# Two causal attentions on one core: GPSIMD masks the diagonal of the first and sums one tile in four of a head of the second

## The reference

```python
xn = layernorm(x)
x = x + attention(xn, wq, wk, wv, wo) + ternary_mlp(xn, W_up, W_gate, W_down)
xn = layernorm(x)
x = x + gated_cumsum(xn, Wq, bq, ...) + attention_two(xn, Wa, Wp, w_std, w_rec)
```

```python
scores = einsum('bhqd,bhkd->bhqk', q, k) * scale
scores = where(causal, scores, -inf)
out    = einsum('bhqk,bhkd->bhqd', softmax(scores), v)
```

## Time and profile before

| what | us |
|---|---|
| median of 3 runs | 2696.15 |
| lowest and highest of them | 2688.54, 2734.21 |
| the profiled execution, its own time | 2693.72 |
| its span, from first to last instruction | 2692.0 |

### The profile page before, as it was taken

The page is one execution under the profiler, slowest core; times in us unless marked ns, Lnnn a source line. Parts: engine busy times, 40 slices in busy tenths (PEclk is TensorE's granted clock), DMA queues, the critical chain, the costliest instruction groups (busy, mean ns, idle before and its releaser), DMA issues. The chain is left out here.

```text
span 2692.0 us, 42224 instructions
## 1 busy us (share of the span) xinstructions
PE 2394.0 (89%) x16394; PEld 1498.7 (56%) x16394; DVE 1749.8 (65%) x2066; ACT 1249.9 (46%) x2372; POOL 566.8 (21%) x480
## 2 busy tenths in 40 slices
PE   4959999969999999999999869979969999999947
PEld 2748888846555444444444347758745555555515
DVE  3745444555767878888886043422259999999954
ACT  2422222204555767777788522212215655656531
POOL 1110000030000000000000002220036766666650
PEclk8979999977999999999999889989989999999978
DMA  3771000034321211000000020015562222220024
GB/s 123 238 231 48 32 32 31 0 62 85 82 61 38 58 45 30 30 30 21 29 18 15 13 67 1 0 48 116 192 145 47 51 65 65 65 63 10 8 67 144
DMA packets 133182, 168.60 MB, mean 63 GB/s; under 512 B 60736, under 2 KB 70592, under 8 KB 129920
## 3 DMA queue, kind: packets, MB, share of 16 engines
q1 hardware_dynamic: 129536, 153.45, 21.5%
q10 hardware_dynamic: 3456, 12.58, 1.5%
HBM read 114.19 MB, written 51.64 MB: 62 GB/s over the span
## 5 line engine op out<-in xcount | busy, mean ns | idle before, releaser
L710 ACT ACTIVATE a_ex<-a_ps_s 128x512 f32<-128x512 f32 (+3 forms) x1280 | 620.0, 532 | 331.3 <-PE a_ps_s L793 249.3
L913 DVE TENSOR_REDUCE a_mx_part<-a_ps 128x2 f32<-128x1024 f32 (+3 forms) x576 | 584.0, 1043 | 132.2 <-PE a_ps L739 129.7
L1206 ACT ACTIVATE a_ex<-a_ps_s 128x512 f32<-128x512 f32 (+3 forms) x640 | 318.3, 532 | 285.9 <-PE a_ps_s L1267 160.3
L793 PE MATMUL a_ps_s<-a_q,a_k 50*128 50x512 f32 (+3 forms) x1152 | 395.9, 419 | 2.8 <-ACT a_ex L710 2.8
L1181 POOL TENSOR_TENSOR a_acc<-a_acc,a_ex 128x512 f32<-128x512 f32 (+3 forms) x288 | 352.0, 1222 | 95.8 <-ACT a_ex L1206 75.0
L739 PE MATMUL a_ps<-a_k,a_q 48*128 48x512 f32 (+3 forms) x1152 | 346.0, 418 | 27.4 <-DVE a_low_q L898 14.8
L837 PE MATMUL a_ps_o<-a_ex,a_v 128*32 128x256 f32 (+1 forms) x5120 | 361.8, 364 | 4.9 <-ACT a_o L680 4.2
L1331 DVE TENSOR_REDUCE a_mx_part<-a_ps 128x2 f32<-128x1024 f32 (+2 forms) x320 | 336.1, 1054 | 32.4 <-PE a_ps L1233 22.8
L793 PEld LDWEIGHTS a_ps_s<-a_q,a_k 50*128 50x128 f32 x1152 | 180.7, 188 | 206.4 <-ACT a_ex L710 144.2
L1230 PE MATMUL a_ps<-a_k,a_q 96*128 96x512 f32 (+3 forms) x640 | 211.6, 397 | 44.1 <-DMA a_q<-q 22.9
L1372 DVE TENSOR_TENSOR a_acc<-a_acc,a_ex 128x512 f32<-128x512 f32 (+3 forms) x288 | 248.8, 864 | 2.3 <-ACT a_ex L1206 0.2
...
## 6 DMA issues: line engine op xcount, KB each, us to landing
a_q<-q SPq DMA_DIRECT2D x192, 64.0 KB, 2.3
...
```

What stands on the lines that cost most here:

```text
L710: act.activation(ex[unit % NE][:, h % 2, off:CH], ps_s[n % 3][:, off:CH], ACT.Exp, scale=SCALE)\
L793: pe.matmul(ps_s[n % 3][:, off:CH], k_st[r0:r0 + KM, g, t * P:(t + 1) * P], q_st[b % NQ][r0:r0 + KM, h // HALVES, off:CH], start=True, sto ...
L913: dve.tensor_reduce(part[:, 2 * p:2 * p + 2, i - TPC * c, kc], bank[:, :, 0:w], AX.X, ALU.max).then_inc(taken1, 1)
L1206: act.activation(ex[s % NE][:, h, off:CH], ps_s[n % 3][:, off:CH], ACT.Exp, scale=SCALE)\
```

## The change

In the first attention the products with `low_k` are gone. The exponentials of a gathered step are taken of unmasked scores, and GPSIMD then sets to zero what lies above the diagonal, in place: one `affine_select` of 128 x 1024 for each pair, 64 in all. `times_v` of a gathered step waits for both. It is done whole at the end of the next step, where before half of it followed each pair. GPSIMD's program is now one by steps: the `divide` of a piece stands two steps, the subtraction five steps behind the step at which its data are loaded, and where a `divide` and a gathered step fall on the same step, the `divide` stands first.

In the second attention 48 of head 1's 320 tiles go from VectorE to GPSIMD, into a total of their own, `acc_lent`: those with `t % 4 == 2` below the diagonal, none in chunk 0, one in chunk 1, two in chunk 2, three in chunk 3 of each group. The first of a run is a copy (24), the others are adds (24). `sums` multiplies a third total by the ones for 24 of the 32 runs. The two rows of maxima get their place in unused partitions of `z_sb`.

```diff
+            def mask_diagonal(s):
+                b, t = STEP_LIST[s]
+                for p in range(PAIRS):
+                    unit = s * PAIRS + p
+                    tiles = ex[unit % NE][:, :, :].rearrange("p e (j q) -> p (e j) q", j=TPC)
+                    pool.wait_ge(exp_done, s * HG + 2 * (p + 1))
+                    pool.affine_select(out=tiles, in_=tiles, compare_op=ALU.is_ge, fill=0.0, base=0,
+                                       pattern=[[0, 2 * TPC], [1, P]], channel_multiplier=-1).then_inc(masked, 1)
...
+            for s in range(STEPS0 + PREP + 5):
+                if s - 5 in PREP_AT:
+                    low(*PREP_AT[s - 5])
+                if s - 2 in PREP_AT:
+                    divide(*PREP_AT[s - 2])
+                if s < STEPS0 and gathered(RUNS[STEP_LIST[s][0]][0], STEP_LIST[s][1]):
+                    mask_diagonal(s)
...
-                sel = mask["k"][0]
-                for part in range(HALVES):
-                    for e in range(2):
-                        r0 = (2 * p + e) % HALVES * ROWS
-                        cols = ps_s[(n + e) % 3][:, :].rearrange("p (j s q) -> p s j q", j=TPC, s=HALVES)[:, part]
-                        mm = pe.matmul(cols, sel[r0:r0 + ROWS, part, :], low_k[r0:r0 + ROWS, :, :],
-                                       start=False, stop=part == HALVES - 1)
...
                 pe.wait_ge(exp_done, (s + 1) * HG)
+                if gathered(c, t):
+                    pe.wait_ge(masked, PAIRS * (b + 1))
...
-                    if s > 0:
+                    if s - 1 in LAST_STEP and p == PAIRS - 1:
+                        times_v(s - 1, 0, CH)
+                    elif s > 0 and s - 1 not in LAST_STEP:
                         times_v(s - 1, p * CH // PAIRS, (p + 1) * CH // PAIRS)
...
+    LENT = [t % TPC == 2 and t < TPC * c for g, c, t in STEP_LIST]
...
+                if LENT[s]:
+                    total, tile = acc_lent[j % 2], ex[s % NE][:, 1, :]
+                    pool.wait_ge(exp_done, (s + 1) * HG)
+                    pool.wait_ge(added0, ADDED0[s] - 1)
+                    if t < TPC:
+                        pool.tensor_copy(total[:, :], tile).then_inc(added0, 1)
+                    else:
+                        pool.tensor_tensor(total[:, :], total[:, :], tile, ALU.add).then_inc(added0, 1)
...
+                if lent:
+                    mm = pe.matmul(ps_1[m % 2][DH:HG * DH, 0, :], one[:, :], acc_lent[j % 2][:, :], start=False, stop=True)
...
-                if 0 <= s - 2 < len(STEP_LIST):
+                if 0 <= s - 2 < len(STEP_LIST) and not LENT[s - 2]:
                     add_ex(s - 2)
```

More of the change, by code:

```diff
@@ L506, in attention @@
         zr = [sb(f"zr{i}", [P, ZN]) for i in range(NZ)]
-        low_k, low_q = [sb(f"low_{n}", [P, TPC, P // HALVES], F32R) for n in "kq"]
+        low_q = sb("low_q", [P, TPC, P // HALVES], F32R)
         o_raw, z_raw = sb("o_raw", [P, CH]), sb("z_raw", [P, CH])
@@ L896, in _ @@
                 dve.memset(part[:, :, :, :], NEG).then_inc(part_init, 1)
-            for n, low in (("k", low_k), ("q", low_q)):
-                dve.tensor_copy(low[:, :, :], mask[n][1][:, :].unsqueeze(1).to_broadcast([P, TPC, P // HALVES]))\
-                    .then_inc(part_init, 1)
-            dve.wait_ge(part_init, 4)
+            dve.tensor_copy(low_q[:, :, :], mask["q"][1][:, :].unsqueeze(1).to_broadcast([P, TPC, P // HALVES]))\
+                .then_inc(part_init, 1)
+            dve.wait_ge(part_init, 3)
             def maxima(n):
@@ L1016, in attention_two @@
     SUMS_ENTRY = {j: sums_entry(n) for n, j in SUMS_AT.items()}
+    LENT = [t % TPC == 2 and t < TPC * c for g, c, t in STEP_LIST]
+    ADDED0 = [s + 1 + sum(LENT[:s + 1]) for s in range(len(STEP_LIST))]
+    ADDED1 = [s + 1 - sum(LENT[:s + 1]) for s in range(len(STEP_LIST))]
     def slots(s):
@@ L1036, in attention_two @@
         acc = [[sb(f"acc{i}_{n}", [P, CH]) for n in range(HG)] for i in range(2)]
+        acc_lent = [sb(f"acc_lent{i}", [P, CH]) for i in range(2)]
         one = sb("one", [P, DH])
@@ L1039, in attention_two @@
         o_sb = [sb(f"o{i}", [OR, CH]) for i in range(2)]
-        z_sb = [sb(f"z_sb{i}", [OR, CH]) for i in range(2)]
+        z_sb = [sb(f"z_sb{i}", [P, CH]) for i in range(2)]
         mx_part = sb("mx_part", [P, HG, QT, NCH])
         mx = [sb(f"mx{i}", [P, HG, TPC]) for i in range(2)]
-        rows = [[sb(f"rows{i}_{s}", [ROWS_F, P], F32R) for s in range(2)] for i in range(2)]
+        rows = [[z_sb[i][OR:OR + ROWS_F, part * P:(part + 1) * P].bitcast(F32R) for part in range(2)] for i in range(2)]
         z = [sb(f"z{i}", [P, ZN]) for i in range(NZ)]
@@ L1092, in put_rows @@
                 for part in range(2):
-                    sp.dma_start(m_d[f, part], rows[b][part][:, :].bitcast(F32)).then_inc(rows_out[b], 16)
+                    sp.dma_start(m_d[f, part], rows[b][part].bitcast(F32)).then_inc(rows_out[b], 16)
                 sp.wait_ge(rows_out[b], 32 * (f // 2 + 1))
@@ L1240, in flip @@
                 pe.wait_ge(taken1, m - 1)
-                pe.matmul(ps_1[m % 2][0:ROWS_F, 0, 0:P], mx[f % 2][:, :, :].rearrange("p h i -> p (h i)"),
+                pe.matmul(ps_1[m % 2][OR:OR + ROWS_F, 0, 0:P], mx[f % 2][:, :, :].rearrange("p h i -> p (h i)"),
                           neg_ident[:, :], start=True, stop=True).then_inc(scores1, 1)
@@ L1248, in sums @@
                 pe.wait_ge(taken1, m - 1)
-                pe.wait_ge(added0, s + 1)
-                pe.wait_ge(added1, s + 1)
+                pe.wait_ge(added0, ADDED0[s])
+                pe.wait_ge(added1, ADDED1[s])
+                lent = j % NCH > 0
                 for h in range(HG):
                     mm = pe.matmul(ps_1[m % 2][h * DH:(h + 1) * DH, 0, :], one[:, :], acc[j % 2][h][:, :],
-                                   start=True, stop=True)
+                                   start=True, stop=h == 0 or not lent)
+                if lent:
+                    mm = pe.matmul(ps_1[m % 2][DH:HG * DH, 0, :], one[:, :], acc_lent[j % 2][:, :], start=False, stop=True)
                 mm.then_inc(scores1, 1)
```

32 lines of the change are left out of this document (18 added, 14 removed).

## The result

| | before | after |
|---|---|---|
| median of the runs on one chip, 4 each (us) | 2699.73 | 2813.58 |
| ratio, 95% interval | | 1.0423 [1.0374, 1.0472] |
| the profiled execution (us) | 2693.72 | 2826.95 |
| first attention, first to last exponential | 934.5 | 1041.0 |
| second attention, the same | 587.2 | 614.8 |

What follows compares the result with a forecast made beforehand. TensorE was taken to set the first attention's pace and VectorE to bound the second. Terms of -1.6 us (first) and -12 us (second) took 2693.7 to 2680.1, a median of 2682 us, range 2652 to 2716.

Steps and rivals of the forecast that it cites:

- It stalls some 0.35 us: First attention, chunk 3: TensorE waits this long for the mask at the moved `times_v`, in about 8 of 32 gathered steps.
- less 0.57 that is E + 1.6, and the mask is hidden: First attention, chunk 2: TensorE reaches `times_v` 1.6 us after E, the gathered step's last exponential's end; no mask wait.
- The mask: First attention: one GPSIMD `affine_select` of 128x1024 takes 1.15 us, carried on from smaller sizes.
- The exponential: First attention, gathered steps: starts 0.29 us sooner without mask products, 0.58 us saved per step, 18.6 us in all.
- The late `divide`: First attention: masks wait behind a `divide` whose data land late, at three early places, together +9 us.
- VectorE is the bound: Second attention: VectorE, busy 293.8 of 299.4 us over four groups, limits the pace, except in the last group's chunks 2 and 3.
- The contention: Second attention: VectorE's remaining adds slow down beside a busier GPSIMD, giving back 25 us (bounds 8 and 58).
- The adds taken: Second attention: 48 adds leave VectorE, 43 of them on the path at 1.035 us each, 44.5 us less.
- The third total: Second attention, `sums`: two more TensorE passes of about 0.6 us each, taken as +3 us, between 0 and 14.
- The last group: Second attention, last group's chunks 2 and 3: GPSIMD, the bound there, gets 2 copies and 3 adds, +4.5 us.
- The late mask: Rival, gathered `times_v`: masks of 2.56 us stall TensorE, first attention 64 us slower, total 2744; chance 0.1.
- The saturated port: Rival, second attention: VectorE's adds cost 1.3 us beside GPSIMD, 42 us come back, total 2697, no change; chance 0.27.

Runs made afterwards that it cites:

- e4: Kernel before with only `times_v` of a gathered step moved behind the next step's scores, mask products kept: first attention 979.4 us, executions 2709 to 2758 us.
- e12: First attention's change alone, plus three dummy products in each run's first step where `times_v`'s first half stood: first attention 959.0 us, ratio 1.009 to before.
- e1: First attention's change alone, second attention as in the kernel before: first attention 1043.0 us, ratio 1.029 to before.
- e6: First attention's change alone, but gathered `times_v` in two halves by head pairs at its old places: first attention 960.9 us, ratio 1.003 to before.
- e14: Kernel before with tiles lent to GPSIMD in the second attention's chunk 2 alone: second attention 593.3 us, ratio 1.002 to before.
- e10: Second attention's change alone, plus six dummy products behind the flip at each group's start: second attention 593.9 us, ratio 1.005 to before.
- e8: Kernel before plus two more passes ahead of the sums of chunks 1 to 3, nothing lent: second attention 598.6 us, ratio 1.004 to before.

## Why the prediction was wrong

**The first attention, the step that failed: "It stalls some 0.35 us", and "less 0.57 that is E + 1.6, and the mask is hidden".** There I followed the moved `times_v` to its new place and counted what it meets. What its old place was left with I didn't ask: the 0.57 us were taken off as if the scores behind them simply came sooner. They came to a wait for VectorE's maxima instead, which grew by about as much (0.37 to 0.80 us in e4). With that place open the clock was at half for 341 us instead of 58, and for the clock the sum has no term. The whole of e4's +45 is in this step, and e12 gets 84 of e1's 108.5 us back by filling the place with dummies. Why the clock falls at some of these places and not at others stays open. The sign was in the rows of before: 0.81 is the granted clock in 600 to 700 us, which I put down to waits behind DMAs alone and priced as waits, not as clock.

**The rest of it was about right.** The mask: 1.10 us for 1.15. The exponential: 0.29 us sooner, as worked out. Eight runs of chunks 1 to 3 at full clock in both kernels are 0.28 us shorter on average, not 0.58: part of the saving ends in other waits, of which the one behind `stage` is shown, the others only argued. The late `divide`: 2.2 us in after, 11.0 in e6, as the data land, forecast 9 (0.6 of it for a third place that none of the rows shows). The sum without the clock is -2.5, forecast -1.6; that these agree is partly luck, as terms on both sides were too large.

**The second attention, the step that failed: "VectorE is the bound".** In chunk 2 of one group of before TensorE is busy 21.14 of 21.64 us and VectorE 21.50. There both are the bound, so what is taken from VectorE can't shorten the chunk by more than TensorE's 0.5 us of room, and what TensorE gets makes it longer:

```profile
2325.12:2346.76 21.64, 21.14 (x127) 11.91 (x126) 21.50 (x34) 13.26 (x26) 15.22 (x13) 1.00 0.27 61
```

I had read the means over four groups, 280.9 of 299.4, as room. *The contention* was sized about right over a group: 4.3 of the 6.2 us came back at once (6.2 - 1.9), where +25 over seven groups is 3.6. In chunk 2 by itself it was nearly all: 1.6 of 2.0 us in e14, 6 x (1.256 - 0.988) for two adds of 0.988. That agrees with the rule of the Trainium skill that I weighed (GPSIMD Engine Reference, Key points), by which GPSIMD and VectorE contend for shared SBUF interfaces; how much comes back the page doesn't say. *The adds taken*: of the 19.5 us that the forecast had left of the 44.5, a group shows 0.3, some 2.6 us in eight. Most of the rest ended in waits: VectorE is idle for 4.0 us of the group in e10, for 2.1 in e8. *The third total*, +3 within 0 to 14, measured 11.4 (e8): in its group 0.84 us in chunk 1, 0.78 in chunk 2 and nothing in chunk 3; why chunk 3 takes its passes for nothing is not shown. *The last group*, +4.5: its chunks 2 and 3 are 3.0 us longer in after, 1.8 in e10. *The clock* had no term: e10 has 51 us less of it at half and is 20.7 us shorter in spite of 8 x 0.3 us of dummies, 0.45 us for each, so the 34 us that came to it over before cost some 15, an estimate. With the passes that is 26.4 of 27.6. Against the forecast of -12 it is 17 us of gain that did not come, 8 of passes and 15 of clock.

**The rivals.** None was this case. The late mask decides from 1.75 us, and it took 1.10. The saturated port came nearest, with no gain in the second attention; but its sign, full adds of VectorE at 1.3 us or more, did not come (1.08 in after, just under the 1.1 to 1.25 forecast), and it named neither TensorE nor the clock. The one on the slower side that was needed, a wait of TensorE that costs its clock, was not among them. Two sums in the working don't come out, and neither moves the forecast: 144 adds at 1.471 give a bound of 63 and not 58 us, and 64 us in the first attention with -12 in the second give 2746 for the late mask and not 2744.
